# Splitting the experts' weights beside attention in 48 half-size parts instead of 24

## What is computed

```python
attn = jnp.einsum('bqhd,bkhd->bhqk', Q, K)
probs = jax.nn.softmax(attn, axis=-1)
ctx = jnp.einsum('bhqk,bkhd->bqhd', probs, V).reshape(bsz * tgt, H)
...
for e in range(E):                     # 8 experts, w1[e] 1024 x 512, w2[e] 512 x 512
    h = x @ w1[e].T + b1[e]
    ...
    ye = y @ w2[e].T + b2[e]
    out = out + ye * we[:, None]
```

## Time and profile before

| | |
|---|---|
| median of 3 runs | 1919.11 us (1914.1 to 1921.01) |
| the profiled execution | 1916.18 us, its span 1914.4 us |
| attention, from about 423 to 1122 us of the span | about 699 us |
| parts split from 445 us (part 0) to 965 us (part 23) | 24 |
| POOL busy in the whole span | 512.1 us (27%) |
| DMA queues: SP's loads and stores (q1) | 205.88 MB, 30.6% of 16 engines' span |
| DMA queues: POOL's (q0) | 79.70 MB, 14.4% |

### The profile page before, as it was taken

How to read it: one execution, slowest core, us unless ns; L and a number is a source line. 1 busy time by engine, 2 the same in 40 slices (tenths; PEclk the granted TensorE clock), 3 DMA queues, 4 the chain that set the end, 5 groups by cost and what they waited for, 6 DMA issues and landing times. The chain is left out here.

```text
span 1914.4 us, 29902 instructions
## 1 busy us (share of the span) xinstructions
PE 1384.7 (72%) x10125; PEld 785.0 (41%) x10245; DVE 1305.3 (68%) x2159; ACT 770.5 (40%) x1459; POOL 512.1 (27%) x325
## 2 busy tenths in 40 slices
PE   0374227733989988988899933458719999999993
PEld 0353103311333433333344410124517777777772
DVE  7975999974877877777788829776454444444441
ACT  4473103320766666666677730002203333333331
POOL 4000015761233343343210001234211233233321
PEclk9876568865999999999999976555559999999997
DMA  4002004664355455545432340101337887888864
GB/s 139 1 1 80 0 1 148 205 211 151 119 189 188 164 183 187 175 170 200 158 110 88 106 157 30 31 28 47 145 151 267 281 280 270 264 264 269 267 186 132
DMA packets 124706, 289.16 MB, mean 151 GB/s; under 512 B 14894, under 2 KB 70062, under 8 KB 114490
## 3 DMA queue, kind: packets, MB, share of 16 engines
q1 hardware_dynamic: 100994, 205.88, 30.6%
q0 software_dynamic: 22592, 79.70, 14.4%
q10 hardware_dynamic: 1056, 2.79, 0.5%
HBM read 201.17 MB, written 92.08 MB: 153 GB/s over the span
## 5 line engine op out<-in xcount | busy, mean ns | idle before, releaser
L1260 DVE TENSOR_REDUCE mxa<-p 128x1 f32<-128x512 f32 x640 | 410.3, 683 | 147.4 <-PE p L1170 93.2
L1287 ACT ACTIVATE pT<-p 128x512 f32<-128x512 f32 x800 | 424.4, 608 | 200.2 <-PE p L1188 196.9
L1170 PE MATMUL p<-ks,qs 128*128 128x512 bf16 x564 | 221.7, 396 | 92.7 <-DMA vs<-d_v 89.8
L1188 PE MATMUL p<-qs,ks 128*128 128x512 bf16 x635 | 244.6, 385 | 27.9 <-ACT pT L1287 12.4
L1206 PE MATMUL p<-pT,vs 128*32 128x128 f32 (+1 forms) x2560 | 209.1, 445 | 1.4 <-ACT pT L1287 1.4
L1792 PE MATMUL p<-x,w 128*128 128x256 bf16 x1728 | 191.6, 273 | 0.0
L1792 PEld LDWEIGHTS p<-x,w 128*128 128x128 bf16 x1728 | 169.1, 98 | 23.4
L1763 POOL DMA_INDIRECT d_acc<-yo,slot_row x54 | 86.7, 1606 | 312.7 <-DMA d_acc<-yo,slot_row 248.1
L1170 PEld LDWEIGHTS p<-ks,qs 128*128 128x128 bf16 x640 | 62.1, 97 | 203.0 <-DMA vs<-d_v 68.5
L1141 POOL CAST xT<-xT 128x2048 bf16<-128x2048 f32 x24 | 45.3, 1886 | 349.7 <-PE p L1206 337.7
L1871 DVE SCALAR_TENSOR_TENSOR sg<-p,b,sg 128x256 f32<-128x256 f32 x108 | 52.3, 484 | 121.7 <-ACT sg L1837 121.6
(11 more groups left out here) (336 smaller groups left out, 2188.3 us busy)
## 6 DMA issues: line engine op xcount, KB each, us to landing
w<-d_w SPq DMA_DIRECT2D x18, 2048.0 KB, 8.5
d_w<-xT POOLq DMA_DIRECT2D x24, 1024.0 KB, 9.4
shared<-d_w SPq DMA_DIRECT2D x9, 2048.0 KB
w<-d_w SPq DMA_DIRECT2D x18, 1024.0 KB, 7.2
xT<-in_w1T POOLq DMA_DIRECT2D x16, 1024.0 KB, 14.5
d_v<-xT SPq DMA_DIRECT2D x20, 512.0 KB, 4.4
vs<-d_v SPq DMA_DIRECT2D x32, 320.0 KB
d_o<-osb SPq DMA_DIRECT2D x32, 320.0 KB, 5.2
```

The source lines that it names most:

```text
L1170: mm = pe.matmul(out, qs[u][:, h, q], ks[u][:, h, 0:512], start=True, stop=True)
L1188: mm = pe.matmul(out, ks[u][:, h, k], qs[u][:, h, 0:512], start=True, stop=True)
L1260: dve.tensor_reduce(mxa[u][:, h, qt:qt + 1], bank, AX.X, ALU.max, negate=True).then_inc(s_mfree, 1)
L1287: act.activation(dst, ps[:, second_bank(c, s)], ACT.Exp).then_inc(s_p, 1)
```

## The change

Each part becomes half a matrix. `HALF` is half of the elements of a part; the load takes two of the four blocks of 128 rows, cast and subtraction work on 1,024 instead of 2,048 elements per partition, and the store writes two runs of 1,024 bfloat16 numbers per partition (one into the `hi` half and one into the `lo` half of the matrix's rows) where it wrote one run of 4,096. There are 48 parts, part n waits for `s_pv` to reach 5n // 2 + 1, so alternately two and three value steps lie between two parts. The two buffers are half as large.

```diff
-        wf = [stage[:, u * IT * L:(u + 1) * IT * L] for u in range(2)]
-        wsplit = [stage[:, (2 + u) * IT * L:(3 + u) * IT * L].bitcast(BF16) for u in range(2)]
+        HALF = IT * L // 2
+        wf = [stage[:, u * HALF:(u + 1) * HALF] for u in range(2)]
+        wsplit = [stage[:, (2 + u) * HALF:(3 + u) * HALF].bitcast(BF16) for u in range(2)]
...
-                sp.wait_ge(s_wst[u], 16 * 3 * EXP_N // 2)
+                sp.wait_ge(s_wst[u], 16 * 3 * EXP_N)
...
-                e, k = divmod(n, 3)
+                (e, k), half = divmod(n // 2, 3), n % 2
                 src = a["w1T"][e, k] if k < 2 else a["w2T"][e]
-                pool.dma_start(wf[n % 2].rearrange("p (i o) -> p i o", i=IT), src.rearrange("(i p) o -> p i o", p=P)
-                               ).then_inc(s_wf[n % 2], 16)
+                pool.dma_start(wf[half].rearrange("p (i o) -> p i o", i=IT // 2),
+                               src.rearrange("(i p) o -> p i o", p=P)[:, half * IT // 2:(half + 1) * IT // 2]
+                               ).then_inc(s_wf[half], 16)
...
-            for n in range(3 * EXP_N):
-                u, (e, k) = n % 2, divmod(n, 3)
-                hi, lo = wsplit[u][:, 0:IT * L], wsplit[u][:, IT * L:]
-                pool.wait_ge(s_pv, SPLIT_PACE * n + 1)
+            for n in range(6 * EXP_N):
+                u, (e, k) = n % 2, divmod(n // 2, 3)
+                hi, lo = wsplit[u][:, 0:HALF], wsplit[u][:, HALF:]
+                pool.wait_ge(s_pv, SPLIT_PACE * n // 2 + 1)
...
-                pool.dma_start(d_w[e, :, k * WPART:(k + 1) * WPART], wsplit[u]).then_inc(s_wst[u], 16)
-                if n + 2 < 3 * EXP_N:
+                pool.dma_start(d_w[e, :, k * WPART:(k + 1) * WPART].rearrange("p (s w) -> p s w", s=2)[
+                    :, :, u * HALF:(u + 1) * HALF], wsplit[u].rearrange("p (s w) -> p s w", s=2)).then_inc(s_wst[u], 16)
+                if n + 2 < 6 * EXP_N:
                     load(n + 2)
```

## The result

| | median us | lowest us | ratio to before [95%] |
|---|---|---|---|
| before, 14 runs beside it | 1919.07 | 1912.78 | |
| after, 14 runs | 1935.63 | 1918.94 | 1.0078 [1.0054, 1.0102] |

The ratio is made from eleven runs of the changed kernel, 1918.94 to 1945.12 us, and twelve of before; of the three left out, one (2567.4 us) was disturbed, while 1956.74 and 1958.24 us have a granted clock of 0.84 like the others and may be the kernel's own spread, and with these two the medians would be 0.9% apart.

What follows compares the result with a forecast made beforehand. Attention's loaded stretch was taken as bound by the work of two DMA engines. The terms -5 + 2.0 + 2.0 - 0.5 gave -1.5 us, so 1917.6 us on the median's scale, with a range of 1900 to 1929.

Steps and rivals of the forecast that it cites:

- The step that failed: Attention's loaded stretch: two hot DMA engines have 21.2 us of work per 20.80 us group, so moving bytes in time changes nothing.
- rival B: Attention's loaded groups: bunched bursts delay the load and smaller ones interleave better; around 1898 us; chance 0.24.
- sign of being wrong: Attention's loaded groups: the prediction fails above all if the two hot DMA engines are idle for part of each period.
- POOL's arithmetic: Splitting on POOL: halved casts and subtractions plus 48 added issues hide behind POOL's waits for PE; cost 0, otherwise 33 us.
- The first loads: Start of attention: 1 MB less passes ahead of group 1; 2.9 to 9 us gained, taken as 5.
- The last parts: End of splitting: half loads run on through group 22, one more loaded group; +2.0 us, at least 0.
- The store's shape: POOL's weight store: runs of 2 KB instead of 8 KB; 0 to +9 us, taken as +2.
- fixed cost near 2 us per DMA: Skill rule against the change: 48 more transfers would cost an estimated 96 us, time 2012; given no weight.
- Rival C: Split store: 2 KB runs cost hot engines over 0.5 us more per matrix; 1928 to 1945, around 1932; chance 0.12.
- The bursts: Loaded groups: gaps between half bursts let the load through; 0 to 42 us gained, taken as 0.5 in total.
- The marks: Attention: PE starts 446 to 451 us, periods 20.5 to 21.1, load waits 30 to 45, end within 5 of 1122.
- main case: Attention's loaded period stays as before; own range 1910 to 1928 us; chance 0.64, including no effect on groups at all.

Runs made afterwards that it cites:

- experiment 2: Kernel before, whole parts, with each group load issued as 12 even pieces of 16 partitions instead of 6; 1869.15 us, ratio 0.9757.
- experiment 3: Changed kernel (halves) with each group load issued as 12 even pieces of 16 partitions instead of 6; 1853.61 us, ratio 0.9681.
- experiment 4: Kernel before with whole parts released two value steps later, at 5n + 3 instead of 5n + 1; 1935.59 us, ratio 1.0105.
- experiment 9: Changed kernel with both halves of a matrix released at value step 5m + 2; 1920.88 us, ratio 1.0027 to the kernel before.
- experiment 10: Kernel before with whole parts released one value step earlier, at 5n; 2011.46 us, ratio 1.0511.
- experiment 11: Changed kernel with the halves released at value steps 5m + 2 and 5m + 3; 1917.44 us, ratio 1.0018 to the kernel before.
- experiment 1: Changed kernel with both halves released at the same value step, where the whole part went before; 1930.9 us, ratio 1.0083 to the kernel before.
- experiment 7: Changed kernel with the second half released one value step behind the first, at 5m + 2; 1936.79 us, ratio 1.0085 to the kernel before.
- experiment 8: Kernel before with whole part 0 held until the second value step of group 0, other parts unchanged; 1912.5 us, ratio 0.9969.
- experiment 5: Kernel before, whole parts, with each 1 MB store made as two transfers of the half parts' shape; 1918.97 us, ratio 1.002.
- experiment 6: Kernel before with whole parts released one value step later, at 5n + 2; 1920.32 us, ratio 1.0015.

## Why the prediction was wrong, point by point

**The step that failed** is the conclusion that attention's loaded stretch is "bound by the work of two DMA engines, not by when that work arrives", and with it the sentence against rival B, that bytes of POOL's "fall on it wherever they are put". The first half was a sound reading: the load's crowding makes all the waits, as experiments 2 and 3 show. The second half did not follow. Experiments 4 and 9 to 11 move the same bytes by 4 to 8 us and the time goes from 1.00 to 1.05. The prediction named its own sign of being wrong, hot engines that are idle for part of each period, and the traces show it where the loss is. At the end of a long group nothing is under way, in after and in the early whole part of experiment 10:

```profile
916.00:918.00 2.00, 1.79 (x15) 0.68 (x16) 2.00 (x4) 2.00 (x5) 1.92 (x2) 1.00 0.00 0
...
600.00:602.00 2.00, 2.00 (x25) 1.08 (x18) 1.55 (x3) 0.84 (x3) 2.00 (x1) 1.00 0.00 0
```

In windows of half a microsecond from 510 to 960 us the DMA share is under 0.06, one engine's worth, for no time at all in before, for 8.5 us in after and for 41 us in experiment 10. So before really was without a gap; the change made the gaps. They are not all of it: 8.5 us is less than a third of what after loses in this stretch, and experiment 4 loses with 1 us of them.

**What happens instead.** The load that PE waits for was issued behind the last store but one, and what counts is how many weight bytes it meets. The transfers of the stretch in which such a load is under way, before from 587 us to its slot at 611.7 (a wait of 3.22 us):

```profile
q1 hardware_dynamic: 1329, 2.22, 27.1%
q0 software_dynamic: 435, 2.25, 25.3%
```

and after, from 917 to 946 us, with the slot at 946.54 (a wait of 7.88):

```profile
q0 software_dynamic: 857, 3.12, 32.1%
q1 hardware_dynamic: 1260, 2.23, 27.3%
```

SP's 2.2 MB are the same. POOL's are 3.12 MB instead of 2.25: the first half starts so soon that a part of the next group's halves falls into the same load too, and the load takes 29.3 us instead of 24.7. At the 5.3 us for 2.1 MB of the prediction, 0.87 MB are 2.2 us of the 4.6; the rest I can't divide up. This pair of loads is no exception. For every load that PE waited for by 0.3 us or more between 510 and 980 us, the traces give POOL's bytes and the time from the store in front of it to PE's slot:

| kernel, loads | POOL's MB met | us, mean (lowest to highest) |
|---|---|---|
| before, 18 | 2.1 to 2.3 | 25.6 (23.8 to 27.0) |
| experiments 9 and 11, 19 and 21 | 2.1 to 2.2 | 25.9 and 26.0 (24.2 to 27.4) |
| after, the 5 with waits over 6 us | 3.1 | 28.8 (28.0 to 29.6) |
| experiments 1 and 7, the 3 and 3 with waits over 6 us | 3.4 to 3.7 | 28.4 and 29.3 (28.1 to 29.7) |
| experiment 10, 9 | 4.2 | 32.8 (31.6 to 33.8) |

Each further megabyte goes with 2 to 4 us. The steps are those of the parts: a load of before has all but landed when the next part's store is issued (20.8 + 4.5 us behind its own issue), one of after has not (18.5 + 1.7 us), and in experiment 10 two whole parts fall into it. The group with the stall gives the load after it more time, which then comes in good time, and the group after that has none: hence the pairs. Shown are the dependence on the first bytes' time (three pairs of kernels, after against 11, 1 against 9 and 7 against 11, and the ruined one) and that loads that meet more bytes take longer; that the pairs keep themselves up in this manner is argued. The Trainium skill (DMA: Bandwidth & Descriptors, on queues, rings and completion order) says that an engine takes packets from its queues in turn. The traces agree: POOL's queue delays SP's without blocking it, by the 25.6, 28.8 and 32.8 us of the table.

**How much of the loss this is.** Moving the first half one step later takes 0.5 to 0.6% off (1.0078 to 1.0027 and 1.0018), 10 to 12 us. Against experiment 8, whole parts with a light start, experiments 9 and 11 are still 0.5 to 0.6% slower, and their 22 loaded groups take 21.15 and 21.03 us where those of experiment 8 take 20.82. The dearer store is the likely ground of that: experiment 5, which has it with whole parts, takes 21.12 us per group in its trace. That the two go together is seen; that one makes the other rests on experiment 5 alone, whose time (1.002) can't be told from none.

**Term by term.**

- *POOL's arithmetic, 0:* right. 48 x (1.03 + 2.13) us, all behind the 261.2 us that POOL still waits for PE. But "cost 0" looked only at whether POOL is late. The halved arithmetic makes the weights' bytes **early**, and that is what cost.
- *The first loads, -5:* right in kind. The first store came 8.05 us earlier in the trace; experiment 8 gets 4 to 6 us from a light start alone.
- *The last parts, +2:* too low. The pairs run on into the group from 983.35 to 1009.86 us, 26.5 us, which is 7.7 more than a free one.
- *The store's shape, +2:* right within its bounds, experiment 5 has +2 to +4. By the fixed cost near 2 us per DMA of the Trainium skill (DMA: Bandwidth & Descriptors, anatomy of one DMA), counted for every transfer, its 24 more would have been an estimated 48 us. Experiment 5 bears out that the prediction gave it no weight. Rival C, whose time (around 1932) is nearest to the measured one, was right in its premise: q0's share of the span is 15.0% x 1943.2 = 291 us for the same bytes against 14.4% x 1914.4 = 276, which is 0.65 us more per matrix and above the 0.5 that C set as its mark, though 6% in all and not a tenth. But it isn't the cause of the loss: experiment 5 has 15.0% x 1921.9 = 288 us, 0.5 us more per matrix, and loses 2 to 4 us, and experiments 9 and 11 have 292 us and lose 3 to 5.
- *The bursts, -0.5:* this is where the time went. Its reason was that 21.2 us of work against 20.80 leaves nothing to gain; its bounds were 0 and a gain, and a loss was not among them. From the first store to the last the changed kernel takes 659.2 us and before 621.0: +38.3 in this execution, of which 4.5 in the first ten groups, 26.4 in the next twelve, 7.4 in the rest; with -8.05 of the start that makes the 30 us at attention's end. The medians' difference is about half of it.

**The marks** set for the main case: PE's start and the shorter second stall came out as said; the period (23.0 us in the later half), the waits for loads (55.9 us), attention's end and q0's share (15.0% of the span instead of 14.4%) did not. Rival B was right that "when" matters. In experiment 3 against 2 its sign and size came out (15.5 us), but the size by luck: B spoke of the crowded load, and what the halves spare there are waits for `nmT`. B took smaller bursts for the virtue and didn't ask where the first of them would lie.

**What stays open.** The strong pairs set in only near 749 us in the trace of after, and its runs spread over 26 us where those of the even loads lie within 9. What tips a run into the pairs wasn't found; experiment 6 has them in its trace and hardly loses. Whole parts with the first bytes at +1.7 us, or halves at 0, were not run, so size and time are separated only by the pairs of kernels above.

## What to carry to other kernels

When a transfer shares crowded DMA engines with a load that the critical engine waits for, compute the issue time of its first byte against that load, and not only the bytes per period: making the work in front of it shorter can move it into the wrong place. Before tuning such timing, look whether the load can be spread over all engines; here that was worth 46 to 61 us where the best timing of the crowded load gave 4 to 6, and it turned the tested change from a loss into a gain. An engine without a gap in the kernel before does not prove that its work is conserved: here the gaps appeared only with the change. And look at PE's granted clock behind each stall: one stall of 4 us cost more than two of 2.

## What was not expected of the hardware

One value step, about 4 us, in the release of a background transfer of 1 MB moved the kernel by 5% to one side and by nothing to the other. With the load issued as 12 even transfers the DMA share over attention rose from 0.47 to 0.67 (windows 423 to 1150 of after and 423 to 1090 of the fastest version) though the kernel asks for the same bytes, and the kernel was still about 4% faster than after (0.9681 against 1.0078): the mean share of 16 engines says little where two of them set the pace.
